# VectorE's work for token chunk 4 is spread between the parts of chunk 3's substitution, in the step in front of the loop

## The reference

```python
sa, ca, ga, sb, cb, gb = (silu(c) @ wmod).reshape(4, 6, 1, 256) ...   # modulation, per batch item
h = layernorm(x) * (1 + ca) + sa                    # x: 4 x 2048 x 256
x = x + ga * attn(h)
h = layernorm(x) * (1 + cb) + sb
x = x + gb * ffn(h)

# attn: 4 heads of 64, chunks of 64 tokens, a decay gamma per head
v  = h @ Ww.T;   rk = h / norm(h, per head);   wk = rk moved on by one token
A  = inv(I + strict_lower(wk wk^T * L))             # 64 x 64, per head and chunk
per chunk, with a state S (64 x 64):
    v_new = A v - (A wk) S
    o     = rk_g S + strict_lower(rk wk^T * L) v_new
    S     = gamma^64 S + wk_g v_new
out = h + (alpha * o) @ Wr.T

# ffn: ternary weights, hidden 1024
h = silu(x w1) * (x w2);  h = gelu(h h1);  h = gelu(h h2);  out = h w3
```

## Time and profile before

| | before |
|---|---|
| median of 3 runs | 1715.2 us (1713.33 to 1718.22) |
| profiled execution, its time | 1712.34 us |
| its span, first to last instruction | 1710.5 us |
| granted clock of TensorE, mean | 0.989 |
| TensorE busy | 1679.5 us (98%) |
| VectorE busy | 1118.3 us (65%) |
| ScalarE busy | 974.2 us (57%) |
| GpSimd busy | 595.9 us (35%) |

### The profile page before, as it was taken

The page is one execution under the profiler, slowest core; times in us unless marked ns, Lnnn a source line. Parts: engine busy times, 40 slices in busy tenths (PEclk is TensorE's granted clock), DMA queues, the critical chain, the costliest instruction groups (busy, mean ns, idle before and its releaser), DMA issues.

```text
span 1710.5 us, 60827 instructions
## 1 busy us (share of the span) xinstructions
PE 1679.5 (98%) x25144; PEld 1613.7 (94%) x25144; DVE 1118.3 (65%) x3167; ACT 974.2 (57%) x2277; POOL 595.9 (35%) x694
## 2 busy tenths in 40 slices
PE   8799999999999999999999999999999999999999
PEld 5598999999999999999999999999999999999998
DVE  5677667667667666667666666766666666676432
ACT  4564555555655555655555665556665555665554
POOL 3544232433332433332343333343333243433111
PEclk8799999999999999999999999999999999999999
DMA  8202223322223222223222223222223332222100
GB/s 283 83 15 39 49 54 57 55 42 51 47 53 61 52 42 52 45 54 61 52 49 48 45 51 60 55 52 42 52 49 56 54 58 42 49 49 48 20 15 13
DMA packets 396496, 92.21 MB, mean 54 GB/s; under 512 B 368372, under 2 KB 388472, under 8 KB 396216
## 3 DMA queue, kind: packets, MB, share of 16 engines
q1 hardware_dynamic: 394224, 85.87, 25.6%
q10 hardware_dynamic: 1992, 2.38, 0.5%
HBM read 45.07 MB, written 30.94 MB: 44 GB/s over the span
## 4 chain that ended last, share of the span: by engine, by line
PE 92%; DVE 1%; ACT 1%; POOL 1%; issue 1%; DMA 0%; SPq 0%; ACTq 0%; DVEq 0%
PE mlp L1214 65%; PE mlp L1288 7%; PE solo L1214 3%; PE duo L1502 3%; PE solo L1371 3%; PE solo L1187 1%; PE duo L1423 1%; PE duo L1491 1%; PE duo L1180 1%; PE duo L1396 1%; PE duo L1175 1%; PE solo L1197 1%; PE duo L1493 1%; PE duo L1383 1%; POOL act_lo L697 1%
## 5 line engine op out<-in xcount | busy, mean ns | idle before, releaser
L1214 PE MATMUL mlp<-act_hi,w_hi 128*128 128x256 f32 x4096 | 970.7, 283 | 2.7 <-POOL act_lo L697 1.5
L1214 PE MATMUL mlp<-act_lo,w_hi 128*128 128x256 f32 x4096 | 949.6, 278 | 0.0
L1214 PEld LDWEIGHTS mlp<-act_hi,w_hi 128*128 128x128 f32 x4096 | 771.3, 188 | 13.2 <-issue 1.7
L1214 PEld LDWEIGHTS mlp<-act_lo,w_hi 128*128 128x128 f32 x4096 | 771.7, 188 | 1.4 <-issue 0.6
L843 ACT ACTIVATE full<-mlp,scale_sb 128x256 f32<-128x256 f32 x512 | 243.4, 475 | 528.1 <-PE mlp L1214 527.9
L933 DVE TENSOR_TENSOR act_lo<-full,act_hi 128x256 fp32r<-128x256 f32 x512 | 251.8, 492 | 313.6 <-ACT act_hi L844 312.2
L697 POOL TENSOR_TENSOR act_lo<-full,act_hi 128x256 fp32r<-128x256 f32 x256 | 186.8, 736 | 485.1 <-ACT act_hi L833 485.1
L844 ACT ACTIVATE act_hi<-mlp,scale_sb 128x256 fp32r<-128x256 f32 x512 | 240.5, 470 | 0.3 <-issue 0.3
L1214 PE MATMUL mlp<-xh,w_hi 128*128 128x256 f32 x768 | 182.7, 280 | 3.3 <-issue 3.3
L1214 PE MATMUL mlp<-xl,w_hi 128*128 128x256 f32 x768 | 181.8, 279 | 0.0
L1065 DVE SCALAR_TENSOR_TENSOR full<-mlp,scale_sb,gate 128x256 f32<-128x256 f32 x192 | 92.9, 484 | 90.8 <-ACT gate L828 88.3
(11 more groups left out here) (184 smaller groups left out, 2634.9 us busy)
## 6 DMA issues: line engine op xcount, KB each, us to landing
w_raw<-in_wts SPq DMA_DIRECT2D x22, 512.0 KB, 5.2
kg<-r SPq DMA_DIRECT2D x64, 126.0 KB
xin<-in_x SPq DMA_DIRECT2D x62, 128.0 KB, 2.8
out_y<-y SPq DMA_DIRECT2D x62, 128.0 KB, 2.5
x_squares<-o_state SPq DMA_DIRECT2D x30, 256.0 KB, 3.2
vn<-x_squares SPq DMA_DIRECT2D x120, 64.0 KB, 2.2
h_squares<-near SPq DMA_DIRECT2D x28, 256.0 KB, 4.3
hT<-h_squares SPq DMA_DIRECT2D x112, 64.0 KB, 2.4
```

The lines of the kernel that those rows point to most:

```text
L1214: mm = pe.matmul(dst, *general_ops, start=is_first and i == 0, stop=is_last and i == 1)
```

## The change

The entries of `third` for chunk 4 (`stats`, `norm`, `square`, `length`, `unit`, `flip`) move to earlier columns, and the parts 1 to 3 of chunk 3's `fs` and its `expand` to later ones. `residual` 0,2 stays where it is. No instruction is added, removed or altered; two lines more of list move the line numbers after it by 2 in the changed kernel.

```diff
--- before.py
+++ after.py
@@ -346,13 +346,15 @@
         ("l3", 7): [("parts", 0, 0), ("silu", 0, 0), ("length", 0, 1), ("n", 2, 0), ("y", 0, 0), ("unit", 0, 1), ("y", 1, 0), ("n", 3, 0)],
         ("l1", 0): [("start", 0, 1)],
         ("l1", 2): [("gram", 0, 1), ("intra", 0, 1)],
-        ("l1", 7): [("solve", 0, 0), ("fs", 0, 1), ("fs", 1, 1)],
-        ("l2", 0): [("old", 0, 0), ("values", 0, 1), ("keys", 0, 0), ("fs", 2, 1)],
-        ("l2", 1): [("solve", 1, 0), ("fs", 3, 1), ("expand", 0, 1), ("stats", 0, 2)],
-        ("l2", 2): [("state", 0, 0), ("norm", 0, 2), ("flip", 0, 2)],
-        ("l2", 3): [("far", 0, 1), ("n", 1, 1), ("square", 0, 2)],
-        ("l2", 4): [("length", 0, 2), ("attn_out", 0, 0)],
-        ("l2", 5): [("n", 2, 1), ("unit", 0, 2), ("flip", 1, 2), ("residual", 0, 2), ("rg", 0, 1)],
+        ("l1", 5): [("stats", 0, 2)],
+        ("l1", 6): [("norm", 0, 2)],
+        ("l1", 7): [("solve", 0, 0), ("fs", 0, 1)],
+        ("l2", 0): [("old", 0, 0), ("values", 0, 1), ("square", 0, 2), ("keys", 0, 0), ("fs", 1, 1), ("flip", 0, 2)],
+        ("l2", 1): [("solve", 1, 0), ("length", 0, 2), ("fs", 2, 1), ("unit", 0, 2)],
+        ("l2", 2): [("state", 0, 0), ("fs", 3, 1), ("expand", 0, 1)],
+        ("l2", 3): [("far", 0, 1), ("n", 1, 1), ("flip", 1, 2)],
+        ("l2", 4): [("attn_out", 0, 0)],
+        ("l2", 5): [("n", 2, 1), ("residual", 0, 2), ("rg", 0, 1)],
         ("l2", 7): [("n", 3, 1)],
     })
```

## The result

| | before | after |
|---|---|---|
| median (11 runs each) | 1714.32 us | 1718.18 us |
| profiled execution, its time | 1712.34 us | 1717.53 us |
| span | 1710.5 us | 1715.7 us |
| granted clock, mean | 0.989 | 0.989 |

The ratio of the times is 1.0022, with a 95% interval from 1.0012 to 1.0031: slower by 2 to 5 us, 3.9 us by the medians. By the medians that is less than the 0.3% that the prediction called no change, and close to its 1718.3 us.

A forecast was written before the change was run, and what follows sets the result against it. TensorE, busy nearly the whole span, was taken as the bound; +5.3 (late `n` 1) - 2.15 - 1.7 (`rT` wait, its low clock) + 1.7 (new low clock) = +3.15 us on a 1715.2 median: 1718.3 us, range 1712.0 to 1722.6.

The forecast's parts named there:

- The hold of product 7: End of `l1`: `norm`, waiting for `rstd`, starts product 7 at 147.56 instead of 143.88; TensorE 3.4 us late.
- the longer price: `norm` between products 6 and 7 takes 2.29 us beside GpSimd's `act_lo`; the other end was 1.8.
- The wait for the inverse: In front of `n` 1: `inv` ready at 161.9, so `n` 1 starts at 162.0, 5.3 us later, 2.5 a new wait.
- a low stretch behind the first is mostly free: Low clock after the first new wait costs little, since `n` 1 waits for VectorE anyway.
- The clock: One low-clock stretch charged, behind the second new wait at 159.5 us: +1.7 us, with 0 as other end.
- The `rT` wait: TensorE's wait at 174.53 us and the low clock behind it go: 2.15 + 1.7, -3.85 us.
- the prediction's own upper end: Upper end of the whole move: +6.2 - 2.15 = +4.05 us, with the added low clock at 0.
- The sum: Whole kernel: +5.3 - 2.15 - 1.7 + 1.7 = +3.15 us, forecast 1718.3 us.
- Works without the price: Rival: `norm`'s hold of product 7 does not reach TensorE; -4.4 us, 1710.8 us; chance 8%.
- The low clock lasts: Rival: clock stays low behind `n` 1, costing 6.9 instead of 1.7 us; +8.35, 1723.6 us; chance 13%.

The follow-up runs named there:

- e1: Changed kernel with `norm` of chunk 4 moved from in front of the product of `l1` column 7 to behind it; ratio to the kernel before 1.0014.
- e6: Kernel before with only `stats` and `norm` moved, between the products of `l1` columns 5, 6 and 7; ratio to the kernel before 1.0009.
- e4: Changed kernel with `rstd` behind the last `act_lo`, `fs` and `expand` at old places, `norm`, `square`, `unit` behind `state`; ratio to the kernel before 0.9988.
- e5: Kernel before with only `fs` 3 and `expand` of chunk 3 moved behind `state` in `l2` column 2; ratio to the kernel before 1.0005.
- e2: Changed kernel with `square`, both flips and `unit` of chunk 4 moved behind the inverse (`expand`); ratio to the kernel before 1.0027.
- e3: Changed kernel with `unit` and its transpose back at their old place behind `n` 2; ratio to the kernel before 1.0028.
- e7: e4 with `unit` and its transpose behind `attn_out` instead of in front; ratio to the kernel before 0.9969, again 0.9973.

## Why the prediction was right, point by point

- **The hold of product 7.** Forecast 147.56, measured 147.33; TensorE 3.4 us late forecast, 3.18 measured, on the path that was named (GpSimd's order, `norm`, rounding, `act_lo`). e1 and e6 show the part by its absence and alone. `norm`'s price was 1.34 + 0.88 again beside GpSimd's `act_lo`, and in e4, with no GpSimd work beside it, the first pair took 0.88: what the Trainium skill says in "SBUF — State Buffer", "Who interferes with whom", holds for these two, and the longer price was the one to take. For GpSimd's `rinv` it does not show (last section).
- **The wait for the inverse.** Forecast: `n` 1 at 162.0, measured 162.73. The sum over VectorE's row was near (10.5 us forecast; it lasted 11.25 us from the first `act_lo` to the end of `inv`), but it passed over two short waits for `act_hi`, 0.18 and 0.67 us. The step "a low stretch behind the first is mostly free" is where they come from: TensorE's columns 1 and 2 came 1.7 us later, and `state` and `fs` 3 are tied to column 2. The prediction also put the wait down to VectorE's load. With TensorE's columns 1 and 2 as late as they came, that part was wrong: e5 shows that the order alone makes 1.7 us, which is all of it, and e2, with 2.9 us less work, has the same wait.
- **The clock.** One stretch was charged, two came. The first was paid in part, through those two waits and a second wait of 1.67 instead of 2.5 us; the second was charged as forecast.
- **The `rT` wait.** It is gone, but this is the term that was mis-sized: -3.85 us was taken as certain from one execution. Three profiles of before give a wait of 0.8 to 2.2 us and the fall of the clock in one. That is 2.2 us on the mean, not 3.85. With the mean of the profiles (118.75 before, 123.9 after) the change costs 5.1 us, outside the prediction's own upper end of 4.05, and by the times 3.9, inside it. How much of the wait the earlier `unit` removed, and how much TensorE's lateness, e3 tells for the short trip alone.
- **The sum.** +3.15 forecast, +3.9 measured. In the first profile the account has 0.8 us more at `n` 1 than forecast, and ends 0.5 us above the 3.4 that the stretch shows. TensorE's starts place that half microsecond: from `n` 1 to `n` 2 the second low stretch costs 1.49 us and not 1.7; from there to `values` it is 0.14 less; with the stall `values` took 2.42 us more and not 2.15; and what follows differs by 1.57 and not by the 1.7 of the old low stretch. 6.07 + 1.49 - 0.14 - 2.42 - 1.57 = 3.43.
- **Luck.** That 1718.3 fell on 1718.18 is luck in part. The forecast stood on a median of 1715.2 from three runs; eleven give 1714.32, and these 0.9 us made up for a move that was 0.7 us larger. And the size of the move rests on a term, `rT`, that one execution happened to show at its largest.
- **The rivals.** "Works without the price" is e4's and e7's kernel, not this one. "The low clock lasts" did not happen: each stretch cost 1.7 us, though it did fall behind each wait.

## What to carry to other kernels

Put work into an engine's gap only if its own inputs are there when the gap begins: `norm` had room for itself and none for the 1.5 us until `rstd`, which GpSimd's queue decided. Take what another engine waits for (here `inv`) out from behind items that are tied to that engine's own progress. And price a DMA wait from several executions before it is booked as a gain; the waits that order makes repeat to the hundredth, this one moved by a factor of nearly three. Nor is a new wait paid out of a later one when what the later one waits for hangs on the engine that is now late: in e5 and e6 `r` left later by nearly as much as TensorE came.

## What the runs showed of the hardware

- The same 256 KB trip through the queue (from the issue of `r_squares` to the next issue, which waits for it) took either 3.2 to 3.4 us or 4.5 to 4.7 us; both came in executions of one kernel (before). The like trip of `h` had two lengths too, but there they went with the kernel in all 13 profiles: 3.3 us in after, e2, e3 and e6, 4.2 to 4.5 us in before, e1, e4, e5 and e7. What chooses between them was not tried.
- Whether the clock falls is not told by the length of a wait alone. It fell behind waits of 2.15 us (before) and 1.67, 1.68 and 1.76 us (after, e2, e3, where another fall lay some 14 us back), and it stayed up behind 1.89 us (before, third profile) and 1.69 us (e5). Each fall cost about 1.7 us.
- GpSimd's power of 8 columns, 2.02 us in the changed profile, ran beside VectorE's `kg` and its `fs` 1, which read two tiles each, and slowed neither:

```profile
153.77 2.02 POOL L636 TENSOR_TENSOR rinv<-ssm,minus_half 128x8 f32<-128x8 f32 x1 [3.19 <-DVE ssm L913]
...
153.60 0.69 DVE L972 TENSOR_TENSOR kg<-kg,tail_decay 128x512 f32<-128x512 f32 x1
...
154.58 0.22 DVE L1006 TENSOR_TENSOR sub_term<-sub_rows,sub 128x56 f32<-128x56 f32 x1
```

  The same product of `fs` 1 took 0.73 us in before, beside GpSimd's decay of `state`.

- The rest of the run drifts. Measured to the `attn_out` of the last chunk, counted from that of chunk 4, the profiles take from 0.2 us less (before, third) to 6.1 us more (e6) than before's first; three profiles of the kernel before differ by up to 1.5 us in it, two of the changed kernel by 0.7. The waits that the profile shows on TensorE do not make it: they add up to 4.0 us in e6 and 4.1 in before. The products of `l1` that read `xh` and `xl` do, at least in part: 281 ns each on the mean in e5 and e6, 276 in before, and there are 1792 of them. Why they take longer, and why e7's times gain more than its profiles, stays open.
